# Two cross-attention layers on one core: a reordered first step, lower parts of the small factors on GpSimd, and a load split in halves around the mix

## The reference

```python
# layer 0, x and y are (32, 128, 1024); H = 8 heads over the 128 rows
q = Wq @ y + bq;  k = Wk @ y + bk;  v = Wv @ x + bv
attn = softmax(q @ k.T / sqrt(128))            # per head 16 x 16
o = Wo @ (attn @ v) + bo + x
x = (o - mean(o)) / sqrt(var(o) + 1e-5) * gn_w + gn_b   # over the whole (128, 1024)
# layer 1, 32 query heads over 8 key heads of 32 columns; W' = W + 2 * (A @ B), rank 16
q = x @ Wq';  k = y @ Wk';  v = y @ Wv'
context = softmax(q @ k.T / sqrt(32)) @ v
out = x + context @ Wo'
```

## Time and profile before

| what | value |
|---|---|
| median of 3 runs | 1324.83 us (1324.82 to 1327.98) |
| the profiled execution | 1328.18 us, its span 1326.2 us |
| PE busy | 1299.6 us, 98% of the span |
| DVE, ACT, POOL busy | 918.8, 828.3, 153.1 us |
| mean granted TensorE clock | 0.988 |
| DMA | 318.67 MB, 239 GB/s over the span |

### The profile page before, as it was taken

How to read it: one execution, slowest core, us unless ns; L and a number is a source line. 1 busy time by engine, 2 the same in 40 slices (tenths; PEclk the granted TensorE clock), 3 DMA queues, 4 the chain that set the end, 5 groups by cost and what they waited for, 6 DMA issues and landing times.

```text
span 1326.2 us, 22899 instructions
## 1 busy us (share of the span) xinstructions
PE 1299.6 (98%) x6824; PEld 1022.6 (77%) x6824; DVE 918.8 (69%) x2037; ACT 828.3 (62%) x2899; POOL 153.1 (12%) x117
## 2 busy tenths in 40 slices
PE   6899999999999999999999999999999999999999
PEld 5677888878788888888888888767767767766767
DVE  4576666666656777777777775687776776766666
ACT  3566666666632777777757776766666666654441
POOL 2344333223210000000000002400000000000000
PEclk7899999999999999999999999999999999999999
DMA  8468777889867887878777888999999899988882
GB/s 283 134 209 289 264 269 255 291 282 299 268 218 211 232 230 227 236 224 227 227 215 224 238 231 273 269 255 250 257 254 263 239 252 258 251 233 230 231 223 93
DMA packets 191785, 318.67 MB, mean 240 GB/s; under 512 B 21136, under 2 KB 85904, under 8 KB 190960
## 3 DMA queue, kind: packets, MB, share of 16 engines
q1 hardware_dynamic: 191664, 317.22, 82.1%
HBM read 232.20 MB, written 84.93 MB: 239 GB/s over the span
## 4 chain that ended last, share of the span: by engine, by line
PE 95%; DVE 2%; issue 1%; ACT 1%; DMA 1%; POOL 0%; SPq 0%; DVEq 0%; POOLq 0%; ACTq 0%
PE bank L647 26%; PE bank L697 23%; PE bank L528 14%; PE bank L718 8%; PE bank L751 5%; PE bank L762 5%; PE bank L600 3%; PE bank L514 2%; PE bank L618 2%; PE bank L503 1%; PE bank L633 1%; PE bank L555 1%; PE bank L572 1%; PE bank L562 1%; PE bank L560 1%
## 5 line engine op out<-in xcount | busy, mean ns | idle before, releaser
L979 ACT ACTIVATE bank<-bank,negs 128x128 f32<-128x128 f32 x1024 | 347.5, 340 | 174.8 <-DVE negs L1254 174.6
L647 PE MATMUL bank<-hT,wq 128*128 128x512 f32 x1488 | 390.3, 400 | 0.0
L697 PE MATMUL bank<-wo,op 128*128 128x512 f32 (+1 forms) x1356 | 345.8, 393 | 0.3 <-issue 0.3
L647 PEld LDWEIGHTS bank<-hT,wq 128*128 128x128 f32 x1488 | 264.0, 189 | 46.3
L697 PEld LDWEIGHTS bank<-wo,op 128*128 128x128 f32 x1356 | 249.6, 189 | 51.8 <-issue 1.5
L1249 DVE TENSOR_REDUCE maxes<-bank 128x4 f32<-128x512 f32 x256 | 175.8, 687 | 133.4 <-PE bank L718 133.2
L996 ACT ACTIVATE probT<-bank 128x512 f32<-128x512 f32 x256 | 152.0, 604 | 113.5 <-PE bank L751 111.8
L528 PE MATMUL bank<-wkv_hi,yT 128*128 128x512 f32 x512 | 210.4, 430 | 7.8 <-POOL wkv_lo L1535 5.1
L979 ACT ACTIVATION_READ_ACCUMULATOR bank<-bank,negs 128x1 f32 x1024 | 209.7, 205 | 0.0
L718 PEld LDWEIGHTS bank<-k_stack,q_stack 96*128 96x128 f32 x1024 | 150.3, 191 | 16.3 <-issue 0.4
L718 PE MATMUL bank<-k_stack,q_stack 96*128 96x128 f32 x1024 | 147.3, 266 | 0.2 <-DMA q_stack<-q_dram 0.2
(11 more groups left out here) (146 smaller groups left out, 1563.7 us busy)
## 6 DMA issues: line engine op xcount, KB each, us to landing
q_stack<-q_dram SPq DMA_DIRECT2D x256, 256.0 KB, 4.0
q_dram<-q_part SPq DMA_DIRECT2D x64, 512.0 KB, 4.1
q_stack<-q_dram SPq DMA_DIRECT2D x256, 128.0 KB, 4.3
yT_in<-in_ctx_turned SPq DMA_DIRECT2D x32, 512.0 KB, 5.0
y_in<-in_ctx SPq DMA_DIRECT2D x32, 512.0 KB, 5.7
x_in<-in_x SPq DMA_DIRECT2D x32, 512.0 KB, 4.3
h_dram<-h_out SPq DMA_DIRECT2D x32, 512.0 KB, 4.3
h_in<-h_dram SPq DMA_DIRECT2D x32, 512.0 KB, 3.6
```

What stands on the lines that cost most here:

```text
L647: m = pe.matmul(bank(u % 2).rearrange("p (a n) -> p a n", a=2), wq[:, block, part, c, :], hT[(group + 1) % 2][:, :, of, c, :], start=c == ...
L697: mm = pe.matmul(place[:, columns], op[m][:, of, c, :], wo[m][w][:, c, columns], start=c == 0 and of == 0 and w == 0, stop=c == GROUP - 1 ...
L979: act.activation(part, part, ACT.Exp, bias=negs[:, n % RING, j:j + 1], scale=SCORE1, accum_out=sums[:, score_column(k), g, j:j + 1]).then_ ...
```

## The change

The head gets another order: ScalarE rounds B of "kv" before A, and A in two halves; VectorE makes the lower part of A's first half and GpSimd that of its second half; merges come before or behind other work of VectorE; `kv_products` takes the chunks in the order 0, 1, 2, 3, 4, 5, 7, 6, and the third VectorE lower part is that of piece 7, not 5. `keep_on` runs 46 transposes at the start (22 before), 6 after the first four products and 6 ahead of `score_product(0)`. The lower parts of A for "q" and "o" move from VectorE to GpSimd: "q" into the head behind GpSimd's weight pieces, "o" into step 2 ahead of `lower_x`. B of "o" goes behind `lower_x` of step 5. `rest_yT(b + 1)` becomes two halves, one ahead of `add_mix(b)` and one behind it, in all steps. `sum_y(b + 1)` comes right behind `softmax0(b)`, `evacuate_n1` and `split_x` come ahead of `prep_round`, and `prep_rest` comes behind `power` and `lower_x`. `split_x(0)` moves from the end of the head into step 1. The load of the "q" factors goes ahead of those of `x` 0 and `y` 1.

```diff
-        LOWER = (1, 3, 5)
+        LOWER = (1, 3, 7)
@@ tensor_program
-            keep_on(22)
+            keep_on(46)
             for n in range(4):
                 prep_product(n)
+            keep_on(6)
             gram_products(0)
+            prep_product(4)
+            prep_product(5)
             turn_gram(0)
-            prep_product(4)
             kv_products(0, (0,))
-            prep_product(5)
+            prep_product(6)
+            kv_products(0, (1,))
+            prep_product(7)
             t1_product(0)
-            kv_products(0, (1,))
-            prep_product(6)
-            kv_products(0, (2,))
-            prep_product(7)
+            kv_products(0, (2, 3))
+            keep_on(6)
             score_product(0)
-            kv_products(0, (3, 4))
+            kv_products(0, (4, 5))
             n1_product(0)
-            kv_products(0, (5, 6))
+            kv_products(0, (7,))
             mix_product(0)
-            kv_products(0, (7,))
+            kv_products(0, (6,))
@@ scalar_program
-            for second in range(2):
-                round_factor("kv", second)
+            round_factor("kv", True)
+            round_factor("kv", False, 0)
+            round_factor("kv", False, 1)
             for half in range(2):
                 round_yT(0, half)
-            begin_gram(0)
             prep_round(0)
             prep_round(1)
+            begin_gram(0)
             prep_round(2)
+            prep_round(3)
             sum_y(0)
+            prep_round(4)
+            prep_round(5)
             scale_bias(0)
-            prep_round(3)
-            prep_round(4)
+            prep_round(6)
+            prep_round(7)
+            round_factor("q", False)
             softmax0(0)
-            prep_round(5)
-            evacuate_n1(0)
-            prep_round(6)
             round_yT(1, 0)
             round_yT(1, 1)
+            evacuate_n1(0)
+            sum_y(1)
             round_mix(0)
-            prep_round(7)
-            sum_y(1)
-            split_x(0)
             evacuate_kv(0)
             for b in range(1, B):
                 begin_gram(b)
                 scale_bias(b)
                 if b == 1:
-                    round_factor("q", 0)
+                    split_x(0)
+                    round_factor("q", True)
...
                 softmax0(b)
+                sum_y(b + 1)
+                evacuate_n1(b)
+                split_x(b)
                 if b > 1 and unit_of(b - 1) < FIRST_O:
                     prep_round(unit_of(b - 1))
-                evacuate_n1(b)
-                split_x(b)
                 round_mix(b)
-                sum_y(b + 1)
+                if b == 5:
+                    round_factor("o", True)
                 evacuate_kv(b)
@@ vector_program
-            lower_a("kv")
+            lower_a_half()
             rest_yT(0, 0)
+            prep_merge(0)
             rest_yT(0, 1)
-            prep_merge(0)
             prep_merge(1)
+            prep_merge(2)
+            prep_merge(3)
             begin_gram(0)
-            prep_merge(2)
+            prep_lower(1)
             finish_gram(0)
-            prep_merge(3)
-            prep_lower(1)
+            prep_merge(4)
+            prep_merge(5)
+            prep_lower(3)
+            prep_merge(6)
+            prep_merge(7)
...
             evacuate_t1(0)
-            prep_merge(4)
-            prep_merge(5)
             softmax0_begin(0)
-            prep_merge(6)
+            prep_lower(7)
             softmax0_end(0)
-            prep_lower(3)
-            prep_merge(7)
-            prep_lower(5)
             rest_yT(1, 0)
+            rest_yT(1, 1)
             add_mix(0)
-            rest_yT(1, 1)
             rest_mix(0)
...
                 partition_stats(b - 1)
-                if b == 1:
-                    lower_a("q")
-                rest_yT(b + 1)
+                rest_yT(b + 1, 0)
                 add_mix(b)
+                rest_yT(b + 1, 1)
...
-                if b == 2:
-                    lower_a("o")
@@ gpsimd_program
             lower_b("kv")
+            lower_a("kv", BANK)
             for n in POOL_LOWER:
                 prep_rest(n)
+            pool.wait_ge(S["wkv_lo_pool"], len(POOL_LOWER))
+            lower_a("q")
             lower_x(0)
             for b in range(1, B):
-                if b in (1, 5):
-                    pool.wait_ge(S["x_lo"], b)
-                    lower_b("q" if b == 1 else "o")
+                if 0 <= b - 2 < LATE_STATS:
+                    power(b - 2)
+                if b == 1:
+                    pool.wait_ge(S["x_lo"], 1)
+                    lower_b("q")
+                if b == 2:
+                    pool.wait_ge(S["pow"], 1)
+                    lower_a("o")
+                lower_x(b)
+                if b == 5:
+                    pool.wait_ge(S["x_lo"], b + 1)
+                    lower_b("o")
                 if b > 1 and unit_of(b - 1) < FIRST_O:
                     prep_rest(unit_of(b - 1))
-                if 0 <= b - 2 < LATE_STATS:
-                    power(b - 2)
-                lower_x(b)
@@ sync_program
             load_yT(1)
+            load_factor("q")
             load_x(0)
             load_y(1)
-            load_factor("q")
```

More of the change, by code:

```diff
@@ L205, in xattn_two_layers @@
             "const", "y_in0", "y_in1", "yT_in0", "yT_in1", "x_in0", "x_in1", "w_raw0", "w_raw1", "first_in", "lora_in_kv", "lora_in_q", "lora_in_o",
-            *(f"wkv_in{i}" for i in range(4)), "lora_a_hi", "lora_b_hi", "lora_a_lo", "lora_b_lo",
+            *(f"wkv_in{i}" for i in range(4)), "lora_a_hi", "lora_b_hi", "lora_a_dve", "lora_a_lo", "lora_b_lo",
             "bq_scaled", "score_bias",
@@ L495, in wait_yT @@
             def wait_yT(b, half):
-                pe.wait_ge(S["yT_lo"], 2 * b + half + 1 if b < 2 else b + 3)
+                pe.wait_ge(S["yT_lo"], 2 * b + half + 1)
             def prep_product(n):
@@ L518, in kv_products @@
             def kv_products(b, chunks):
+                final = NC - 1 if b else NC - 2
                 for c in chunks:
@@ L528, in kv_products @@
                         m = pe.matmul(bank(2), yT[b % 2][:, c, part, :], w[:, c, :], start=first,
-                                      stop=c == NC - 1 and part == 1)
-                    if c == NC - 1:
+                                      stop=c == final and part == 1)
+                    if c == final:
                         m.then_inc(S["kv_mm"], 1)
@@ L853, in scalar_program, with round_factor @@
         def scalar_program(act):
-            def round_factor(m, second):
-                of = slice(HID, HID + COLS[m]) if second else slice(0, HID)
+            def round_factor(m, second, half=None):
+                if second:
+                    of = slice(HID, HID + COLS[m])
+                else:
+                    of = slice(0, HID) if half is None else slice(half * BANK, (half + 1) * BANK)
                 act.wait_ge(S[f"lora_in_{m}"], DMA)
@@ L1094, in vector_program, with lower_a_half, rest_yT @@
         def vector_program(dve):
-            def lower_a(m):
-                dve.wait_ge(S["lora_a_hi"], MODULES[m])
-                dve.tensor_tensor(lora[m][A_LOWER, 0:HID], lora_raw[m][A_LOWER, 0:HID], f32(lora[m][A_LOWER, 0:HID]),
-                                  ALU.subtract).then_inc(S["lora_a_lo"], 1)
-            def rest_yT(b, half=None):
+            def lower_a_half():
+                of = slice(0, BANK)
+                dve.wait_ge(S["lora_a_hi"], 1)
+                dve.tensor_tensor(lora["kv"][A_LOWER, of], lora_raw["kv"][A_LOWER, of], f32(lora["kv"][A_LOWER, of]),
+                                  ALU.subtract).then_inc(S["lora_a_dve"], 1)
+            def rest_yT(b, half):
                 if b >= B:
                     return
-                dve.wait_ge(S["yT_hi"], b + 3 if half is None else 2 * b + half + 1)
+                dve.wait_ge(S["yT_hi"], 2 * b + half + 1 if b < 2 else b + 3)
                 of = yT_chunks(half)
@@ L1563, in power, with lower_a @@
                 pool.tensor_tensor(rstd, ve, minus_half[:], ALU.pow).then_inc(S["pow"], 1)
+            def lower_a(m, first=0):
+                of = slice(first, HID)
+                pool.wait_ge(S["lora_a_hi"], {"kv": 2, "q": 3, "o": 4}[m])
+                pool.tensor_tensor(lora[m][A_LOWER, of], lora_raw[m][A_LOWER, of], f32(lora[m][A_LOWER, of]),
+                                   ALU.subtract).then_inc(S["lora_a_lo"], 1)
+                pool.wait_ge(S["lora_a_lo"], MODULES[m])
             def lower_b(m):
```

16 lines of the change are left out of this document (7 added, 9 removed).

## The result

| | before | after |
|---|---|---|
| median, same job | 1325.38 us (1324.82 to 1327.98, 4 runs) | 1313.65 us (1310.50 to 1317.60, 4 runs) |
| profiled execution | 1328.18 us, span 1326.2 | 1317.60 us, span 1315.6 |

The ratio is 0.990, 95% interval [0.988, 0.992]: 1% faster, about half of what was forecast (1301), and outside the range of 1295 to 1310.

What follows compares the result with a forecast made beforehand. The loop was taken as bound by TensorE. Gains of 8.7 + 4.5 + 1.2 + 1.1 + 1.3 + 8.1 = 24.9 us gave 1303.3 profiled; 24 off the median gave 1301, range 1295 to 1310.

Steps and rivals of the forecast that it cites:

- the steady step: Loop: an undisturbed step falls from 10.53 to 10.25 us as `prep_product` no longer waits for `xbias`.
- another wait: Rival, loop: mix or ScalarE is late by as much, the steady 8.1 us is lost: 1309, chance 0.12.
- the rival that was slower: Rival, loop: `rest_mix` loses the port to `x_lo`, TensorE waits about 1.5 us a step: 1343, chance 0.07.
- the term: Steps 2 to 30: halves of `rest_yT` around the mix gain 0.28 us a step, 8.1 in 29 steps.
- the head: Start of the kernel: step 1's Gram product begins at 26.8 us, gain 8.7, bounds 4.5 to 11.8.
- the rival of a late clock: Rival, head: port blocks pile up or the clock rises late; step 1 begins near 31 us: 1305, chance 0.12.
- The 20.6 us: Head before the change: time read as spent at the lower clock, out of the first 35.49 us.
- the block: Head: VectorE's `prep_lower(7)` waits behind GpSimd's 2.38-us "q" factor, costing its remaining 1.8 us.
- The low clock for what is left: End of the head: TensorE's last products, n1, mix and evacuations at the lower clock take 3.3 us.
- step 1: Step 1: the 4.5-us stall goes, smaller waits come, among them `lower_x(1)` holding the port: 12.65 us, gain 4.5.
- `prep_rest` behind `lower_x`: Loop: SyncE's stores and loads slip some 6 us but stay covered; cost nothing, bounds 0 and 0.5 a step.
- B("o") behind `lower_x`: Step 5: the excess of steps 5 and 6 (1.18 and 0.11) goes, gain 1.3 us.

Runs made afterwards that it cites:

- e5: The kernel before with only the lower part of the turned context made in halves around `add_mix`: 1320.46 us, ratio 0.994.
- e12: The changed kernel with `rest_yT` in one piece, the weight piece's lower part ahead of `power` and `lower_x`, and y summed last: 1315.18 us, ratio 0.991.
- e8: The changed kernel with A("q") made by GpSimd in step 1 behind `lower_x(0)` instead of in the head: 1308.95 us, ratio 0.986.
- e4: The changed kernel with `rest_yT` in one piece ahead of `add_mix` again: 1315.62 us, ratio 0.991.
- e1: The changed kernel with `prep_rest` ahead of `power` and `lower_x` again, and ScalarE's old order with it: 1309.38 us, ratio 0.986.
- e2: The changed kernel with SyncE's stores of h, keys and values ahead of its wait for the query weight piece (steps 2 to 17): 1308.19 us, ratio 0.986.
- e10: e6 and e8 together, and `lower_x(1)` waits for the second half of `rest_yT(2)`: 1303.21 us, ratio 0.982.
- e11: Like e10, but with `prep_rest` late and SyncE's stores of h, keys and values ahead of the wait for it: 1304.32 us, ratio 0.983.
- e6: The changed kernel with the edits of e1 and e3 together: 1306.91 us, ratio 0.984.
- e3: The changed kernel with SyncE's store of the merged "o" piece and next weight load ahead of the x and y loads (steps 18 to 31): 1309.90 us, ratio 0.988.

## Why the prediction was wrong, point by point

**Right: the steady step.** Forecast 10.25, measured 10.24 to 10.27. At the end of step 6, an undisturbed one, the lines that answer to the earlier trace rows:

```profile
89.27 0.68 DVE L1116 TENSOR_TENSOR yT<-yT_in,yT 128x512 fp32r<-128x512 f32 x1
...
90.06 0.15 DVE L1206 TENSOR_TENSOR norm<-bank,first 128x1 f32<-128x1 f32 x1
...
90.40 0.39 PE L532 MATMUL bank<-wkv_hi,yT 128*128 128x512 f32 x1
90.63 0.39 PE L506 MATMUL bank<-lora_q 96*128 96x512 f32 x1
90.86 0.39 PE L532 MATMUL bank<-wkv_hi,yT 128*128 128x512 f32 x1
...
91.17 0.28 DVE L1210 TENSOR_TENSOR mix_split<-mix,mix_split 128x128 fp32r<-128x128 f32 x1
```

`xbias` ends at 90.21, 0.42 ahead of `prep_product` (0.35 was forecast), and from the matmul ahead to the one behind it is 0.46, the pair's 0.47 of the earlier trace rows. So the rival "another wait" falls. `rest_mix` takes 0.28 and `lower_x` comes 0.31 behind it: the rival that was slower falls too, in steps like this one. What the term left out is what 29 shorter steps take from the loads (below): the profile of e5, which has it alone, shows 5.8 of the 8.1.

**Right in size, in part by luck: the head.** 27.27 against 26.8. The first product comes at 9.22, not 8.4, because the 46 transposes end there; the lower parts of B and of A's first half were ready at 8.1 and 8.7. The transposes' pace doubles at 7.10 in this trace (26 of them in 5.59 us up to there, 0.215 each, then 0.11) and at 4.50 in that of before (14 in 2.98), though TensorE turns without a gap from 1.5 on in both; so 24 more of them cost more than the 0.11 each that was taken, as the rival of a late clock had it, by 0.8 us. (The clock column says 1.00 for these stretches: the trace's clock record begins at the first rise, so the pace is what shows the level. The 20.6 us that the prediction read from the earlier trace rows are some 3 short for the same reason.) Over the profiles of this study the pace doubles between 4.5 and 7.7, and of the kernels with the new head e12, where it comes first of all, has the latest Gram product of step 1 (27.99): the moment of the rise doesn't decide the head.

```profile
1.51 7.95 PE L773 MATMUL bank<-ident 128*128 128x128 f32 x46 [1.51 <-POOL ident L1525]
9.22 1.17 PE L506 MATMUL bank<-lora_kv 96*128 96x512 f32 x4
...
17.44 1.23 DVE L1422 SCALAR_TENSOR_TENSOR score_bias<-first,bq_scaled,score_bias 128x128 f32<-128x128 f32 x1
20.59 0.68 DVE L1401 TENSOR_TENSOR wkv_lo<-wkv_raw,wkv_hi 128x512 fp32r<-128x512 f32 x1
21.02 2.46 POOL L1575 TENSOR_TENSOR lora_q<-lora_raw_q,lora_q 32x1024 fp32r<-32x1024 f32 x1 [1.22 <-ACT lora_q L866]
21.50 2.06 DVE L1200 TENSOR_SCALAR att<-att,att_stat 128x128 f32<-128x128 f32 x1
...
23.71 0.46 PE L571 MATMUL bank<-first,att 128*128 128x128 f32 x2 [2.55 <-DVE att L1200]
```

`score_bias` is blocked as forecast (1.23). `prep_lower(7)` is not: it takes 0.68 at 20.59, ahead of the "q" factor. But the next instruction, the softmax's last multiplication, takes 2.06 beside it, and TensorE waits 2.55 for that: the block was forecast on the right piece of GpSimd and on the wrong instruction of VectorE, with n1 at 23.71 for 23.5. The low clock for what is left came as well, from 24.17, but in only four of the nine profiles with this piece; without it the forecast of 26.8 would have met a start near 26. e8 takes the piece away and gains the 2.2.

**Right, placed one step late: step 1.** The 4.5-us stall is gone. `lower_x(1)` does hold the port against the second half of `rest_yT(2)`, and the next Gram product waits 0.65 for it, inside step 2:

```profile
37.72 2.62 DVE L1116 TENSOR_TENSOR yT<-yT_in,yT 128x512 fp32r<-128x512 f32 x1
...
40.39 0.74 PE L517 MATMUL bank<-yT 128*128 128x256 f32 x4 [0.65 <-DVE yT L1116]
```

So step 1 is 0.8 shorter than forecast and step 2 is 0.8 longer. The excess of steps 3 and 5 is gone but for 0.36 in step 3.

**The step that failed: "`prep_rest` behind `lower_x`. [...] the load is now issued near 14 and I give it 3; [...] 3 us of cover. The others have 3 to 5. Cost nothing, bounds 0 and 0.5 a step."** It named the right queue, and the last sentence of the prediction even named SyncE's loads as a releaser of ScalarE as what would make it wrong. The cover was mis-sized, twice; part of the second cost belongs to the halves.

*The key store* had no 3 to 5. In the trace of before, the store of the keys of element 7 is issued at 128.75 and lands at 132.68; the copy of element 9, which waits for it, starts right after step 10 does, at 141.0: 8.3 of slack. After the change, the store in the same place is issued 4.93 behind the next step's start instead of 1.47 ahead of it, 6.4 later, and two steps take 0.56 off: 8.3 - 6.4 - 0.56 = 1.3. The trace of after agrees: issued at 120.41, landed at 124.64, copied at 125.99.

```profile
120.41 1.04 SPq L1681 DMA_DIRECT2D k_dram<-kT_sb  x1
...
125.99 0.37 ACT L961 COPY kv_sb<-bank 128x256 f32<-128x256 f32 x1 [1.11 <-PE bank L532]
```

1.3 is less than this store's own scatter: it takes 4.2 us to land in a quiet step and 6.29 at 161.38, which is the stall of step 14. And B("o"), which the change places ahead of the piece in step 5, is 2.4 more: step 7. The prediction costed `prep_rest` behind `lower_x` and B("o") behind `lower_x` as two edits; it never put them on one queue. Cost: 5.4 us in steps 7, 14, 16 and 18.

*The weight load* doesn't take 3 us everywhere. It did in the steps where it was read, but in the loop's last steps it takes twice that. From the listing of DMA issues of the kernel before, between 331 and 356 us (count, KB each, median us to landing), and its waits from 325 to 378:

```profile
w_raw<-in_w_units SPq DMA_DIRECT2D x3, 256.0 KB, 6.2
```

```profile
DVE w_raw L1117 <- DMA w_raw<-in_w_units: 1.2, 1, 1.2
```

VectorE of the kernel before already stood 1.2 us for this load in step 30 (11.61 us), and TensorE 0.4 behind it. That row was there to be read and said that the cover in this stretch was below zero; a change that shortens steps lengthens that wait. So step 30 isn't the late piece's doing: e4, which has that piece without the halves, makes it 11.67, e5, which only shortens the steps, 12.90, and e1, where the piece is early, 12.75; after makes it 14.66, of which 1.7 is a tail at the lower clock. It is a cost of the halves that stood nowhere in the sum. In step 19 the load is issued at 213.63 behind x and y loads that SyncE gave out late, lands 9.3 later, and VectorE stands 2.33 for it. This one does come from the late piece: in e1 and e2, which leave the weight load where it is, step 19 has no stall.

```profile
213.63 0.50 SPq L1660 DMA_DIRECT2D w_raw<-in_w_units  x1
...
222.95 0.69 DVE L1127 SCALAR_TENSOR_TENSOR w_raw<-bank,w_raw 128x512 f32<-128x512 f32 x1 [2.33 <-DMA w_raw<-in_w_units]
...
224.31 0.46 PE L559 MATMUL bank<-first,gram 128*128 128x128 f32 x2 [1.62 <-DVE gram L1138]
```

Cost: 2.2 in steps 19 and 22 and 3.3 more than before in step 30. Both terms together are 10.9 of the 12.7 us by which steps 2 to 30 missed the forecast; of the rest 0.8 is step 2 (above) and 1.1 lies in steps 3, 24, 25 and 29, which are as long in e10 and e11. In the trace of e10 TensorE waits there for `lower_x(2)` (step 3) and for VectorE (0.2 each in steps 25 and 29); what makes VectorE late is open.

Had these terms stood in the sum, it would have been 1303.3 + 11 = 1314 for the profiled execution, which took 1317.60; the rest is the 1.8 just named and the 2.0 of the second stage. With both orders mended (e6) the change is worth 21.8 of the 24 that were taken from the median; e10 and e11, which also mend the head, 24.4 and 23.3.

**Open.** Step 31 and the second stage take 1 to 4 us longer in the profiles of after and of all variants (963.8 to 967.3, before 963.06), e5 among them, which only has the halves. One wait there grows, TensorE's first for `q_stack`, from 0.2 in before to 0.9 in after and 2.3 in e2. Why was not tried.

## What to carry to other kernels

When work is moved later on an engine, follow every queue that waits for it to the end of the chain and subtract: landing time and next use of each transfer, from rows, with the spread of its landing time and not its best. A wait that already shows in one step of the kernel before says that the cover there is below zero, and a shorter loop eats cover everywhere by its own gain. In a queue that is issued in order, a wait belongs behind everything that doesn't need it: here the order of three entries in SyncE's list was worth some 5 us. Two transfers that add to one semaphore are waited for together, even where only the earlier one matters.

## What the runs showed of the hardware

A VectorE multiplication of one SBUF tensor by a per-partition scalar (128x128) takes 0.29 us alone and 2.06 beside a GpSimd subtraction (1.85 in step 1): it ended at 23.56, right behind GpSimd's 23.48, and so took turns with GpSimd like the operations with two tensor operands, of which alone the prediction thought. The Trainium skill (SBUF — State Buffer, "SBUF: two separate sides") counts VectorE operations in a two-port performance mode among those that contend for the lock, beside those with two SBUF inputs. The trace agrees in that this operation with one tensor input was blocked; in which mode it ran, no run shows. In e8 the same instruction runs clear of GpSimd:

```profile
21.59 0.29 DVE L1200 TENSOR_SCALAR att<-att,att_stat 128x128 f32<-128x128 f32 x1
```

The same stall of TensorE doesn't cost the same twice. In step 7 of after it stood 1.76 and then ran 3.4 us at the lower of its two levels. In step 7 of e3 it stood 2.0 at the same place and the clock did not fall:

```profile
91.55:103.93 12.38, 10.39 (x57) 8.49 (x56) 7.26 (x25) 7.00 (x15) 4.14 (x4) 1.00 1.01 356
```

In step 30 the same: behind stops of 1.9 in after and 2.1 in e2 and e8 the clock fell (14.66 to 14.92), behind 1.5 in e1 and 1.7 in e5 it did not (12.75 and 12.90). A stall's price was its length or twice that, so a sum that ends in a short stop has to carry both.
